# Quantizing the gate and up weights inside the attention stage, in tiles of 1024 columns, instead of in a stage of their own

## The chip, the cores and the metric

The kernel runs on all 8 cores of one Trainium2 chip. Each core takes half of one batch element: 1024 rows of the output, with the other 1024 rows of its batch element as keys and values. All weights are given to every core, and every core does all the weight preparation for itself. The metric is the device time of the slowest core in microseconds. Of the kernel before there are three timed runs (60560.01, 60564.8 and 60569.77 us, median 60564.8 us) and one profiled execution.

TensorE (PE in the profile) multiplies matrices and transposes, VectorE (DVE) and ScalarE (ACT) work element by element, GpSimd (POOL) and SyncE (SP) only issue DMAs here. Each engine works through its own queue in program order.

## The reference

A layer norm of x gives xn, then two branches are added to x:

```
q, k, v = xn @ Wq.T + bq, ...              # 16 heads of 256
logits  = (q_rev*met) @ k.T / 16 + (q_rev @ wk[h]) @ k.T
attn    = softmax(logits) @ v
gate    = mxq(xn, 3 bits) @ mxq(w_gate, 1 bit).T      # w_gate, w_up: [11008, 4096]
up      = mxq(xn, 3 bits) @ mxq(w_up, 1 bit).T
ffn     = mxq(silu(gate)*up, 3 bits) @ mxq(w_down, 1 bit).T
y       = x + attn + ffn
```

`mxq` works on blocks of 32 values along the contraction: it finds the largest magnitude of a block, takes the power of two below it as a shared scale, and rounds each scaled value to the nearest of a few values (0, 0.5, 1, 1.5, 2, 3, 4, 6 with a sign for 1 bit of mantissa). Since a block has 32 values, a row can be quantized in pieces of any multiple of 32 columns.

## The kernel before

There are four stages, with a barrier of all engines and queues between them. Their places on the time axis are those of the slowest core.

- **Stage 1** (to about 1600 us, lines 260 to 349): layer norm of 16 tiles of 128 rows; each tile is transposed into `s_xnT` in DRAM. For the core's own 8 tiles, `_emit_quant` also quantizes the row in two pieces of 2048 columns, with the working tiles `QT` (`q_...` in the profile).
- **Stage 2** (to about 15280 us, lines 351 to 526): the attention, one head at a time. A head first casts its q, k and v weights on DVE (12 casts of 128x2048, from the double-buffered `wstage`). Then comes a loop over four slices of 512 positions (`tc`): PE multiplies the `xnc` tiles with the weights, 32 steps to a slice, ACT evicts `kh` and `qtmp`, DVE evicts `vh`. PE then makes `qeff`. Then comes a loop over 8 tiles of 128 queries (`qt`): logits on PE, maximum (`nm`) on DVE, exponential on ACT, transposes on PE, copies on DVE, product with v on PE, and a scaled copy to `ostg` on DVE, which POOL stores into `s_attn`.
- **Stage 3** (to about 42340 us, lines 528 to 594): the weights. For each 128-row tile of `wg` and `wu` (86 row tiles each, 4096 columns) and of `wd` (32 row tiles, 11008 columns), pieces of 2048 (for `wd` 2752) columns of float32 are loaded by SP into one of two `win` tiles, quantized by `_emit_quant` on DVE and ACT into `wqrt`, transposed by PE in batches of 8 blocks of 128x128, copied by DVE from PSUM to `tstg3`, and stored by POOL.
- **Stage 4** (lines 596 to 736): gate and up products, silu, quantization of the product in 1024 columns (working tiles `QT4`, `f_...` in the profile), transposes, and the down product, four times for 256 rows.

The order of the work on an engine is the order in which the Python code emits it. `Eng.op` (line 31) lets each instruction of DVE, ACT and PE wait for the one before it on its own engine, so there is no overlap of two instructions within an engine. `Stream.dma` (line 50) issues a DMA on SP or POOL; `qwait` (line 232) puts a wait into the queue of SP or POOL, and everything that is emitted later on that queue stays behind it.

`_emit_quant` (line 100) with `mbits` 1 is, on DVE: a block maximum, 50 small instructions on one value for each block, a multiplication into `zt`; then ACT makes `sgn` and `at` (absolute value) from `zt` while DVE waits; then 11 more instructions on DVE over all columns. Only `sgn`, `at` and `zt` tie it to ACT.

Of the kernel before, what the change touches and what calls it, by code (L numbers as in the profile page):

```python
# [7 lines left out]
F32 = mybir.dt.float32  # L8
BF16 = mybir.dt.bfloat16
# [4 lines left out]
D = 4096  # L14
# [4 lines left out]
I = 11008  # L19
# [161 lines left out]
def build_nc():  # L181
# [18 lines left out]
    s_wgT = nc.dram_tensor("s_wgT", [D, I], BF16, kind="Internal").ap()  # L200
    s_wuT = nc.dram_tensor("s_wuT", [D, I], BF16, kind="Internal").ap()
    s_wdT = nc.dram_tensor("s_wdT", [I, D], BF16, kind="Internal").ap()

    ctx = ExitStack()
    with ctx:
# [3 lines left out]
        def sem(name):  # L209
            return ctx.enter_context(nc.semaphore(name))  # L210
# [50 lines left out]
        with p1:  # L261
            def sb1(name, shape, dt=F32):
                return p1.enter_context(nc.sbuf_tensor(name, shape, dt))
# [4 lines left out]
            xnq_t = sb1("xnq_t", [128, D], BF16)  # L268
            tstage = [sb1("tstage%d" % i, [128, 1024], BF16) for i in range(2)]
            psT = [p1.enter_context(nc.psum_tensor("psT%d" % i, [128, 1024], BF16)) for i in range(2)]  # L270
            QT = {
                "am": sb1("q_am", [128, 64], F32), "b1": sb1("q_b1", [128, 64], F32),
                "b2": sb1("q_b2", [128, 64], F32), "b3": sb1("q_b3", [128, 64], F32),
                "b4": sb1("q_b4", [128, 64], F32), "b5": sb1("q_b5", [128, 64], F32),
                "zt": sb1("q_zt", [128, 2048], F32), "at": sb1("q_at", [128, 2048], F32),
                "u2": sb1("q_u2", [128, 2048], F32),
                "cA": sb1("q_cA", [128, 2048], BF16), "cB": sb1("q_cB", [128, 2048], BF16),
                "cC": sb1("q_cC", [128, 2048], BF16), "cD": sb1("q_cD", [128, 2048], BF16),
                "cE": sb1("q_cE", [128, 2048], BF16), "cF": sb1("q_cF", [128, 2048], BF16),
                "sgn": sb1("q_sgn", [128, 2048], BF16),  # L280
            }

            t.wait(lds.sem, small_ld)
            xnT_v = s_xnT.rearrange("p (a c) -> p a c", a=32)
# [24 lines left out]
            for tt in range(NTILE):  # L309
                par = tt % 2  # L310
                qwait(nc.sync, ssem, buf_free[par])
                ldm = ldx[par].dma(xt2[par][:], xb[tt*128:(tt+1)*128, :])
                v.wait(ldx[par].sem, ldm)
                s.wait(ldx[par].sem, ldm)
                v.op("reduce_sum", lnS[:], xt2[par][:], AX.X)
                s.op("activation", sqscr[:], xt2[par][:], ACT.Square, accum_out=lnQ[:])
                sqm = s.n
                v.wait(ssem, sqm)
                v.op("tensor_single_scalar", lnM[:], lnS[:], 1.0 / D, ALU.mult)
                v.op("tensor_single_scalar", lnE[:], lnQ[:], 1.0 / D, ALU.mult)  # L320
# [12 lines left out]
                s.op("activation", xnf[:], xt2[par][:], ACT.Identity, bias=lnB[:], scale=lnR[:])
                s.op("activation", xnb[:], xnf[:], ACT.Identity)
                buf_free[par] = s.n
                xnm = s.n
                t.wait(ssem, xnm)
                emit_transpose_out(xnb, xnT_v, tt)
                if tt < NOWN:
                    v.wait(ssem, xnm)  # L340
                    for cc in range(2):
                        _emit_quant(v, s, xnf[:, cc*2048:(cc+1)*2048], 2048, 3, QT,
                                    xnq_t[:, cc*2048:(cc+1)*2048])
                    xqm = v.n
                    t.wait(vsem, xqm)
                    emit_transpose_out(xnq_t, xnqT_v, tt)
# [5 lines left out]
        with p2:  # L352
# [47 lines left out]
            for h in range(NH):  # L400
# [3 lines left out]
                for wname, wview, wbuf in (("q", wqT_v, wq_bf), ("k", wkT_v, wk_bf), ("v", wvT_v, wv_bf)):  # L404
# [8 lines left out]
                        wfree_v[wp] = v.n  # L413
                    wcast[wname] = v.n
                t.wait(vsem, max(wcast.values()))
                for tc in range(4):
                    for dc in range(32):
                        par = dc % 2
# [35 lines left out]
                    evV = v.n  # L454
                    t.wait(ssem, evK)
                    t.wait(vsem, evV)
                for cc in range(2):
                    for nn in range(2):
                        t.op("matmul", ps[0][:], th_all[:, h*128:(h+1)*128],
                             qtmp[:, cc*LQ + nn*512: cc*LQ + nn*512 + 512], start=True, stop=True)  # L460
                        trm = t.n
                        s.wait(tsem, trm)
                        s.op("activation", qeff[:, cc*LQ + nn*512: cc*LQ + nn*512 + 512],
                             ps[0][:], ACT.Identity)
                        t.wait(ssem, s.n)
                qeffm = s.n
                t.wait(ssem, qeffm)
                for qt in range(8):
                    for kc in range(4):
                        for cc in range(2):  # L470
# [37 lines left out]
                    for kc in range(16):  # L508
# [10 lines left out]
                    sto[opar].dma(s_attn[qt*128:(qt+1)*128, h*HD:(h+1)*HD], ostg[opar][:])  # L519
                    pmark[("ost", opar)] = sto[opar].cnt  # L520
                    pmark["attn_cons"] = t.n
                pmark["kh_cons"] = t.n
            p2_marks = [(vsem, v.n), (ssem, s.n), (tsem, t.n),
                        (ldw[0].sem, ldw[0].cnt), (ldw[1].sem, ldw[1].cnt), (ld2s.sem, ld2s.cnt),
                        (ldc[0].sem, ldc[0].cnt), (ldc[1].sem, ldc[1].cnt),
                        (sto[0].sem, sto[0].cnt), (sto[1].sem, sto[1].cnt)]

        p3 = ExitStack()
        with p3:
# [21 lines left out]
            psT3_free = [0, 0]  # L551
            qcons = 0

            for wdram, wscr, R, Cw in ((wg, s_wgT, I, D), (wu, s_wuT, I, D), (wd, s_wdT, D, I)):
                csz = 2752 if Cw % 2752 == 0 else 2048
                wscr_v = wscr.rearrange("(a p) c -> p a c", p=128)
                for rt in range(R // 128):
                    for cc in range(Cw // csz):
                        par = (rt * (Cw // csz) + cc) % 2
                        qwait(nc.sync, vsem, in_free[par])  # L560
                        ldm = ld3[par].dma(win[par][:, 0:csz], wdram[rt*128:(rt+1)*128, cc*csz:(cc+1)*csz])
                        v.wait(ld3[par].sem, ldm)
                        s.wait(ld3[par].sem, ldm)
                        def qg(qcons=qcons):
                            v.wait(tsem, qcons)
                        _emit_quant(v, s, win[par][:, 0:csz], csz, 1, QT3,
                                    wqrt[:, cc*csz:(cc+1)*csz], qgate=qg)
                        in_free[par] = v.n
                    qdone = v.n
                    t.wait(vsem, qdone)  # L570
                    nk = Cw // 128
                    for batch in range((nk + 7) // 8):
                        bpar = batch % 2
# [23 lines left out]
        with p4:  # L597
            def sb4(name, shape, dt=F32):
# [4 lines left out]
            wsl = [sb4("wsl%d" % i, [128, 32 * 512], BF16) for i in range(2)]  # L603
            sgt = sb4("sgt", [128, 1024], F32)
            intf = sb4("intf", [128, 1024], F32)
            QT4 = {
                "am": sb4("f_am", [128, 32], F32), "b1": sb4("f_b1", [128, 32], F32),
                "b2": sb4("f_b2", [128, 32], F32), "b3": sb4("f_b3", [128, 32], F32),
                "b4": sb4("f_b4", [128, 32], F32), "b5": sb4("f_b5", [128, 32], F32),
                "zt": sb4("f_zt", [128, 1024], F32), "at": sb4("f_at", [128, 1024], F32),  # L610
                "u2": sb4("f_u2", [128, 1024], F32),
                "cA": sb4("f_cA", [128, 1024], BF16), "cB": sb4("f_cB", [128, 1024], BF16),
                "cC": sb4("f_cC", [128, 1024], BF16), "cD": sb4("f_cD", [128, 1024], BF16),
                "cE": sb4("f_cE", [128, 1024], BF16), "cF": sb4("f_cF", [128, 1024], BF16),
                "sgn": sb4("f_sgn", [128, 1024], BF16),
            }
# [30 lines left out]
            for tt2 in range(4):  # L647
# [4 lines left out]
                for ici in range(NIC):  # L652
# [31 lines left out]
                    ev_marks["mul"] = v.n  # L684
                    def qg4():
                        v.wait(tsem, iq_free)
                    _emit_quant(v, s, intf[:, 0:2*isz], 2 * isz, 3, QT4, iq[:, 0:2*isz], qgate=qg4)
                    iqm = v.n
                    t.wait(vsem, iqm)
                    t.wait(vsem, psTr_free)  # L690
# [99 lines left out]
```

How the kernel before makes its waits and increments, by code:

```python
    def op(self, method, *args, **kw):  # L31
        if self.n > 0:
            self.e.wait_ge(self.sem, self.n)
        inst = getattr(self.e, method)(*args, **kw)
        inst.then_inc(self.sem, 1)
        self.n += 1
        return inst
# [1 line left out]
    def wait(self, sem, count):  # L39
        if count > 0:
            self.e.wait_ge(sem, count)
# [8 lines left out]
    def dma(self, out, in_):  # L50
        self.q.dma_start(out=out, in_=in_).then_inc(self.sem, 16)
        self.cnt += 16
        return self.cnt
# [1 line left out]
    def dmaT(self, out, in_):  # L55
        self.q.dma_start_transpose(out=out, in_=in_).then_inc(self.sem, 16)
        self.cnt += 16
        return self.cnt
# [122 lines left out]
def build_nc():  # L181
# [50 lines left out]
        def qwait(q, semh, val):  # L232
            if val > 0:
                q.wait_ge(semh, val)
# [490 lines left out]
                        v.wait(sty[ypar].sem, yst_free[ypar])  # L725
                        v.op("tensor_tensor", yst[ypar][:], psD[tc][:], xres[:], ALU.add)
                        v.op("tensor_tensor", yst[ypar][:], yst[ypar][:], ares[:], ALU.add)
                        res_free = v.n
                        ym = v.n
                        qwait(nc.gpsimd, vsem, ym)
                        sty[ypar].dma(y[row0:row0+128, dcD*512:(dcD+1)*512], yst[ypar][:])
                        yst_free[ypar] = sty[ypar].cnt
                    t.wait(vsem, res_free)
                iqT_free = t.n
            nc.sync.wait_ge(sty[0].sem, sty[0].cnt)
            nc.sync.wait_ge(sty[1].sem, sty[1].cnt)
    return nc
```

## Time and profile before

| | |
|---|---|
| median of three runs | 60564.8 us |
| the profiled execution's own time | 60516.05 us |
| its span on the slowest core (core 0) | 60515.0 us |
| spans of the eight cores | 60432.7 to 60515.0 us |
| granted TensorE clock, all cores | 1.000 |
| DVE busy | 23785.4 us, 39% |
| PE busy | 20771.3 us, 34% |
| ACT busy | 3052.9 us, 5% |
| POOL busy | 1114.4 us, 2% |
| HBM traffic | 41 GB/s over the span |

No engine is busy most of the time, and the memory is far from busy. The work is a chain: an instruction ends, the next one on the same or another engine starts. The share of busy time of an engine says little here; what counts is which engine holds the chain in a given stage. Line 34 is the helper `Eng.op`, so nearly all instructions have that line, and the profile is read by tile names. Line 51 is the helper that issues DMAs.

### The profile page before, as it was taken

Reading aid. Unit: us, or ns where it says so; the run is one execution under the profiler, and the core shown is the slowest. Engines: PE = TensorE matmul, PEld = TensorE weight load, DVE = VectorE, ACT = ScalarE, POOL = GpSimd, SP = SyncE. Lnnn points to the kernel's source line nnn. Section 1 sums busy time; section 2 is a strip of 40 time slices with the busy share of each in tenths; the row PEclk is TensorE's granted clock in tenths of the full one; section 3 lists DMA queues with packets and bytes.
Section 4 is the critical chain, followed back from the end, with each engine's and each line's share of the span. In section 5 each row is a group of like instructions: output and inputs, shape, how many; then the busy total and the mean of one; then the engine's idle time right before and its main releaser. Section 6 shows DMA issues by size and latency. Waiting matters only on the chain.

```text
span 60515.0 us, 254596 instructions; the slowest of 8 cores (60432.7 to 60515.0 us)
## 1 busy us (share of the span) xinstructions
PE 20771.3 (34%) x46000; PEld 4828.0 (8%) x46000; DVE 23785.4 (39%) x41288; ACT 3052.9 (5%) x2691; POOL 1114.4 (2%) x1332
## 2 busy tenths in 40 slices
PE   1666666666100000000000000000555555555555
PEld 0111111111000000000000000000100001001101
DVE  6000000000666666666666777766220220220220
ACT  1000000000000000000000000000000000000000
POOL 0000000000000000000000000000000000000000
DMA  1111111111000100000011111111112112112212
GB/s 36 43 36 37 32 40 35 37 37 32 28 29 29 29 29 29 29 29 29 29 29 29 31 32 32 31 33 34 63 56 66 64 59 66 64 59 67 66 56 68
DMA packets 1823659, 2516.91 MB, mean 42 GB/s; under 512 B 114464, under 2 KB 1662752, under 8 KB 1759648
## 3 DMA queue, kind: packets, MB, share of 16 engines
q1 hardware_dynamic: 1720608, 2171.28, 11.3%
q0 software_dynamic: 101632, 329.34, 2.2%
q8 instruction: 570, 9.34, 0.1%
q14 instruction: 849, 6.96, 0.0%
HBM read 2170.90 MB, written 329.25 MB: 41 GB/s over the span
## 4 chain that ended last, share of the span: by engine, by line
DVE 38%; PE 33%; issue 16%; DMA 7%; ACT 5%; DVEq 1%; SPq 0%; ACTq 0%; POOL 0%; POOLq 0%
PE ps L34 12%; DVE p_b L34 9%; DVE p_cB L34 8%; DVE p_cA L34 7%; DMA wdsl<-s_wdT 5%; PE psT L34 4%; PE psQ L34 3%; PE psD L34 3%; PE psA L34 3%; PE psC L34 3%; PE psB L34 3%; PE psDD L34 3%; DVE p_zt L34 2%; DVE wqrt L34 2%; DVE p_am L34 2%
## 5 line engine op out<-in xcount | busy, mean ns | idle before, releaser
L34 PE MATMUL psT<-idn_sb,wqrt 128*128 128x128 bf16 x8256 | 2171.8, 263 | 24890.2 <-DVE wqrt L34 23679.8
L34 PE MATMUL psD<-wdsl,iqT 128*128 128x512 bf16 x5504 | 3213.4, 584 | 2481.2 <-DMA wdsl<-s_wdT 1697.9
L34 DVE TENSOR_TENSOR vh<-ps,bv_sb 128x256 bf16<-128x256 f32 x256 | 108.8, 425 | 8855.2 <-PE psQ L34 5164.4
L34 DVE SCALAR_TENSOR_TENSOR p_cA<-p_at,p_cA 128x2048 bf16<-128x2048 f32 (+1 forms) x1416 | 3527.1, 2491 | 150.4 <-DVE p_cA L34 4.1
L34 PE MATMUL ps<-wv_bf,xnc 128*128 128x256 bf16 x8192 | 3031.0, 370 | 1229.5 <-PE ps L34 101.6
L34 DVE TENSOR_TENSOR intf<-sgt,psC 128x512 f32<-128x512 f32 x88 | 59.5, 676 | 8320.5 <-ACT sgt L34 8320.5
L34 PEld LDWEIGHTS psT<-idn_sb,wqrt 128*128 128x128 bf16 x8256 | 866.6, 105 | 26195.5 <-issue 26195.5
L34 PE MATMUL ps<-xnc,wk_bf 128*128 128x512 bf16 x4096 | 2388.2, 583 | 1575.1 <-DVE wv_bf L34 802.5
L34 DVE TENSOR_SCALAR p_b<-p_b 128x64 f32<-128x64 f32 (+1 forms) x11800 | 2340.3, 198 | 1297.0 <-DVE p_b L34 62.6
L34 DVE TENSOR_TENSOR p_b<-p_b 128x64 f32<-128x64 f32 (+1 forms) x9912 | 2296.9, 232 | 1070.7 <-DVE p_b L34 54.7
L34 DVE TENSOR_TENSOR yst<-psD,xres 128x512 f32<-128x512 f32 x64 | 44.3, 692 | 5629.5 <-DMA ares<-s_attn 4261.3
L34 ACT ACTIVATE p_sgn<-p_zt 128x2048 bf16<-128x2048 f32 (+1 forms) x472 | 976.2, 2068 | 25017.9 <-DVE p_zt L34 25017.9
L34 DVE COPY tstg<-psT 128x1024 bf16<-128x1024 bf16 (+1 forms) x1040 | 714.9, 687 | 2929.7 <-PE psT L34 2927.6
L34 PE MATMUL psA<-wsl,xnq_tt 128*128 128x512 bf16 (+1 forms) x2816 | 1614.8, 573 | 549.7 <-PE psA L34 125.3
L34 PE MATMUL psDD<-wsl,xnq_tt 128*128 128x512 bf16 (+1 forms) x2816 | 1614.5, 573 | 423.3 <-PE psDD L34 131.5
L34 PE MATMUL psB<-wsl,xnq_tt 128*128 128x512 bf16 (+1 forms) x2816 | 1614.5, 573 | 423.3 <-PE psB L34 131.8
L34 PE MATMUL psC<-wsl,xnq_tt 128*128 128x512 bf16 (+1 forms) x2816 | 1614.5, 573 | 423.3 <-PE psC L34 129.9
L34 PE MATMUL psTr<-idn_sb,iq 128*128 128x128 bf16 x688 | 181.2, 263 | 4013.8 <-DVE iq L34 3923.7
L34 DVE TENSOR_SCALAR p_cA<-p_at 128x2048 bf16<-128x2048 f32 (+1 forms) x472 | 626.1, 1326 | 2153.4 <-ACT p_at L34 2153.4
L34 PE MATMUL psQ<-xnc,wq_bf 128*128 128x512 bf16 x2048 | 1194.0, 583 | 307.5 <-PE psQ L34 50.6
L34 DVE TENSOR_TENSOR p_zt<-win,p_b 128x2048 f32<-128x2048 f32 (+1 forms) x472 | 1176.0, 2491 | 52.7 <-DVE p_b L34 5.0
L34 DVE SCALAR_TENSOR_TENSOR p_cB<-p_cA,p_cB 128x2048 bf16<-128x2048 bf16 (+1 forms) x472 | 1175.6, 2491 | 51.6 <-DVE p_cC L34 3.2
(138 smaller groups left out, 21055.7 us busy)
## 6 DMA issues: line engine op xcount, KB each, us to landing
wdsl<-s_wdT SPq DMA_DIRECT2D x2752, 128.0 KB, 2.2
wsl<-s_wgT SPq DMA_DIRECT2D x84, 4096.0 KB, 13.7
wsl<-s_wuT SPq DMA_DIRECT2D x84, 4096.0 KB, 13.6
xnc<-s_xnT SPq DMA_DIRECT2D x2048, 128.0 KB, 2.0
win<-wg SPq DMA_DIRECT2D x172, 1024.0 KB, 5.0
win<-wu SPq DMA_DIRECT2D x172, 1024.0 KB, 5.0
win<-wd SPq DMA_DIRECT2D x128, 1376.0 KB, 5.6
s_wgT<-tstg POOLq DMA_DIRECT2D x344, 256.0 KB, 3.2
```

Of the source, the lines that this page charges most:

```text
L34: inst = getattr(self.e, method)(*args, **kw)
```

## The change

Stage 3 for `wg` and `wu` is split in two. Their quantization moves into stage 2, as 688 tasks of 128x1024 (86 row tiles x 4 pieces x 2 matrices), whose results go to two new DRAM tensors `s_wgq` and `s_wuq`. Stage 3 then loads a quantized row of bfloat16 straight into `wqrt` and only transposes it. The tasks are emitted by `qtask(n)`: four before a head's loop over `tc`, three after the evictions of each slice, two before its loop over `qt`, one after the store of `ostg` of every odd query tile, and all that are left after the last head. `wd` keeps its old path. The 1024-column working tiles `QTG` replace `QT` and `QT4`, so stage 1 quantizes in four pieces of 1024 columns instead of two of 2048; stage 4 does what it did, in the new tiles.

```diff
+        qld = [Stream(nc.gpsimd, sem("qld%d" % i)) for i in range(2)]
+        qst = [Stream(nc.gpsimd, sem("qst%d" % i)) for i in range(2)]
...
+        def qtask(n):
+            for _ in range(n):
+                ti = qstate["i"]
+                if ti >= len(wq_tiles):
+                    return
+                qstate["i"] += 1
+                wdram_, wscr_, rt_, cc_ = wq_tiles[ti]
+                par = ti % 2
+                qwait(nc.gpsimd, vsem, qstate["in_free"][par])
+                ldm = qld[par].dma(win2[par][:],
+                                   wdram_[rt_*128:(rt_+1)*128, cc_*1024:(cc_+1)*1024])
+                v.wait(qld[par].sem, ldm)
+                s.wait(qld[par].sem, ldm)
+                def qg(par=par):
+                    v.wait(qst[par].sem, qstate["st_mark"][par])
+                _emit_quant(v, s, win2[par][:], 1024, 1, QTG, qsg[par][:], qgate=qg)
+                qstate["in_free"][par] = v.n
+                qwait(nc.gpsimd, vsem, v.n)
+                qst[par].dma(wscr_[rt_*128:(rt_+1)*128, cc_*1024:(cc_+1)*1024], qsg[par][:])
+                qstate["st_mark"][par] = qst[par].cnt
...
-                    for cc in range(2):
-                        _emit_quant(v, s, xnf[:, cc*2048:(cc+1)*2048], 2048, 3, QT,
+                    for cc in range(4):
+                        _emit_quant(v, s, xnf[:, cc*1024:(cc+1)*1024], 1024, 3, QTG,
...
                 t.wait(vsem, max(wcast.values()))
+                qtask(4)
...
                     t.wait(vsem, evV)
+                    qtask(3)
...
                 t.wait(ssem, qeffm)
+                qtask(2)
...
+                    if qt % 2 == 1:
+                        qtask(1)
                 pmark["kh_cons"] = t.n
+            qtask(len(wq_tiles))
...
+                qwait(nc.sync, tsem, qcons)
                 for rt in range(R // 128):
...
+                    if prequant:
+                        par = rt % 2
+                        qwait(nc.sync, tsem, qcons)
+                        ldm = ld3[par].dma(wqrt[:, 0:Cw], wdram[rt*128:(rt+1)*128, :])
+                        t.wait(ld3[par].sem, ldm)
```

The first place is the queue of POOL in the first head: before, the stores of `ostg` stand one behind the other.

```order
100 L51 DMA s_attn<-ostg0 128x256 [waits vsem,ssem,tsem,lds,ldx0,ldx1,stt0,stt1]
101 L51 DMA s_attn<-ostg1 128x256 [waits vsem]
102 L51 DMA s_attn<-ostg0 128x256 [waits vsem]
103 L51 DMA s_attn<-ostg1 128x256 [waits vsem]
104 L51 DMA s_attn<-ostg0 128x256 [waits vsem]
```

Now the same queue holds the loads (`win2`) and the stores (`qsg`) of the tasks; these rows are the last tasks before the query loop of the first head, and the first task within it.

```order
131 L51 DMA s_wgq<-qsg1 128x1024 [waits vsem]
132 L51 DMA win2_0<-wg 128x1024 [waits vsem]
133 L51 DMA s_wgq<-qsg0 128x1024 [waits vsem]
134 L51 DMA win2_1<-wg 128x1024 [waits vsem]
135 L51 DMA s_wgq<-qsg1 128x1024 [waits vsem]
136 L51 DMA s_attn<-ostg0 128x256 [waits vsem]
137 L51 DMA s_attn<-ostg1 128x256 [waits vsem]
138 L51 DMA win2_0<-wg 128x1024 [waits vsem]
139 L51 DMA s_wgq<-qsg0 128x1024 [waits vsem]
140 L51 DMA s_attn<-ostg0 128x256 [waits vsem]
```

The load of a task stands behind the store of the task before it, which waits for DVE to finish that task.

The second place is DVE at the end of the last slice of the first head and at the first query tile. Before, the maximum follows the eviction of `vh`.

```order
1434 L34 TENSOR_TENSOR vh<-ps4,bv_sb 128x256
1435 L34 TENSOR_TENSOR vh<-ps5,bv_sb 128x256
1436 L34 TENSOR_REDUCE nm<-ps0 128x1
1437 L34 TENSOR_REDUCE nm<-ps1 128x1
1438 L34 TENSOR_REDUCE nm<-ps2 128x1
```

Now five tasks stand between them (61 rows each; the first and the last row of the outer ones are shown), and one task stands between `ostg` of an odd query tile and the maximum of the next.

```order
3364 L34 TENSOR_TENSOR vh<-ps5,bv_sb 128x256 [waits vsem]
3365 L34 TENSOR_REDUCE g_am<-win2_1 128x32 [waits qld1,vsem]
...
3609 L34 TENSOR_REDUCE g_am<-win2_1 128x32 [waits qld1,vsem]
...
3669 L34 TENSOR_TENSOR qsg1<-g_cB,g_b5 128x1024 [waits qst1,vsem]
3670 L34 TENSOR_REDUCE nm<-ps0 128x1 [waits tsem,vsem]
...
3693 L34 TENSOR_SCALAR ostg1<-ps5,rr 128x256 [waits tsem,vsem]
3694 L34 TENSOR_REDUCE g_am<-win2_0 128x32 [waits qld0,vsem]
...
3754 L34 TENSOR_TENSOR qsg0<-g_cB,g_b5 128x1024 [waits qst0,vsem]
3755 L34 TENSOR_REDUCE nm<-ps0 128x1 [waits tsem,vsem]
```

So 60 instructions or more of DVE now stand where nothing stood. A head has 4 + 4x3 + 2 + 4 = 22 tasks, so the 16 heads take 352 of the 688; the last call takes the other 336, with no other work beside them.

## Rows read from the trace of the kernel before

**Rows 1.** The page: the span, and the costliest wait of a group.

```profile
span 60515.0 us, 254596 instructions; the slowest of 8 cores (60432.7 to 60515.0 us)
...
L34 PE MATMUL psT<-idn_sb,wqrt 128*128 128x128 bf16 x8256 | 2171.8, 263 | 24890.2 <-DVE wqrt L34 23679.8
```

**Rows 2.** Busy time by stretch, us (instructions): stage 2, then stage 3's gate and up.

```profile
1600.00:15260.00 13660.00, 8535.04 (x19490) 2045.95 (x19490) 1099.24 (x2301) 569.60 (x1281) 74.22 (x127) 1.00 0.12 36
15260.00:33870.00 18610.00, 1454.57 (x5523) 579.71 (x5523) 12786.48 (x22361) 1313.52 (x688) 607.92 (x687) 1.00 0.10 29
```

**Rows 3.** Timeline, DVE, one gate row tile: start us, duration us, instruction.

```profile
20039.83 2.29 DVE L34 TENSOR_REDUCE p_am<-win 128x64 f32<-128x2048 f32 x1
...
20131.19 2.29 DVE L34 TENSOR_TENSOR wqrt<-p_cB,p_b 128x2048 bf16<-128x2048 bf16 x1
...
20147.96 2.29 DVE L34 TENSOR_REDUCE p_am<-win 128x64 f32<-128x2048 f32 x1
```

**Rows 4.** Timeline, PE, first and last of the 32 transposes of a row tile.

```profile
20025.71 0.26 PE L34 MATMUL psT<-idn_sb,wqrt 128*128 128x128 bf16 x1 [95.04 <-DVE wqrt L34]
...
20038.53 0.26 PE L34 MATMUL psT<-idn_sb,wqrt 128*128 128x128 bf16 x1 [0.15 <-PE psT L34]
```

**Rows 5.** Timeline, DVE, a 1024-column quantization of stage 4.

```profile
45030.10 1.22 DVE L34 TENSOR_REDUCE f_am<-intf 128x32 f32<-128x1024 f32 x1
...
45049.97 0.69 DVE L34 TENSOR_SCALAR f_cA<-f_at 128x1024 bf16<-128x1024 f32 x1 [2.52 <-ACT f_at L34]
45050.77 0.69 DVE L34 TENSOR_SCALAR f_cB<-f_at 128x1024 bf16<-128x1024 f32 x1
...
45052.10 1.23 DVE L34 SCALAR_TENSOR_TENSOR f_cC<-f_cB,f_cC 128x1024 bf16<-128x1024 bf16 x1
45053.43 1.23 DVE L34 TENSOR_TENSOR f_u<-f_at,f_cC 128x1024 f32<-128x1024 f32 x1
...
45070.45 1.23 DVE L34 TENSOR_TENSOR iq<-f_cD,f_b 128x1024 bf16<-128x1024 bf16 x1
```

**Rows 6.** Timeline, DVE, one head of stage 2.

```profile
4199.33 2.56 DVE L34 CAST wq_bf<-wstage 128x2048 bf16<-128x2048 f32 x2
...
4243.42 1.23 DVE L34 CAST wv_bf<-wstage 128x2048 bf16<-128x2048 f32 x1 [1.48 <-DMA wstage<-wvT]
4405.46 2.01 DVE L34 TENSOR_TENSOR vh<-ps,bv_sb 128x256 bf16<-128x256 f32 x4 [160.81 <-PE psQ L34]
...
4686.47 2.01 DVE L34 TENSOR_TENSOR vh<-ps,bv_sb 128x256 bf16<-128x256 f32 x4 [115.03 <-PE ps L34]
4803.55 2.01 DVE L34 TENSOR_TENSOR vh<-ps,bv_sb 128x256 bf16<-128x256 f32 x4 [115.07 <-PE ps L34]
4818.17 3.07 DVE L34 TENSOR_REDUCE nm<-ps 128x1 f32<-128x512 f32 x4 [12.62 <-PE ps L34]
...
4842.09 0.48 DVE L34 TENSOR_SCALAR ostg<-ps,rr 128x256 f32<-128x256 f32 x1 [8.78 <-PE ps L34]
4847.89 3.08 DVE L34 TENSOR_REDUCE nm<-ps 128x1 f32<-128x512 f32 x4 [5.31 <-PE ps L34]
```

**Rows 7.** Timeline, POOL, the store of that `ostg`.

```profile
4843.11 0.54 POOL L51 DMA_DIRECT2D s_attn<-ostg  x1 [642.43 <-DVE ostg L34]
```

**Rows 8.** DMA issues: count, KB each, median us from issue to landing.

```profile
xnc<-s_xnT SPq DMA_DIRECT2D x2048, 128.0 KB, 2.0
win<-wg SPq DMA_DIRECT2D x172, 1024.0 KB, 5.0
...
xres<-xb SPq DMA_DIRECT2D x64, 256.0 KB, 3.1
...
y<-yst POOLq DMA_DIRECT2D x64, 256.0 KB, 4.1
```

**Rows 9.** Timeline, DVE, two quantizations of stage 1, one after the other.

```profile
42.56 2.29 DVE L34 TENSOR_REDUCE q_am<-xnf 128x64 f32<-128x2048 f32 x1
...
105.58 2.29 DVE L34 TENSOR_REDUCE q_am<-xnf 128x64 f32<-128x2048 f32 x1
```

More of the change, by code:

```diff
@@ L202, in build_nc @@
     s_wdT = nc.dram_tensor("s_wdT", [I, D], BF16, kind="Internal").ap()
+    s_wgq = nc.dram_tensor("s_wgq", [I, D], BF16, kind="Internal").ap()
+    s_wuq = nc.dram_tensor("s_wuq", [I, D], BF16, kind="Internal").ap()
     ctx = ExitStack()
@@ L253, in build_nc @@
         rr = sb("rr", [128, 1], F32)
+        QTG = {
+            "am": sb("g_am", [128, 32], F32), "b1": sb("g_b1", [128, 32], F32),
+            "b2": sb("g_b2", [128, 32], F32), "b3": sb("g_b3", [128, 32], F32),
+            "b4": sb("g_b4", [128, 32], F32), "b5": sb("g_b5", [128, 32], F32),
+            "zt": sb("g_zt", [128, 1024], F32), "at": sb("g_at", [128, 1024], F32),
+            "u2": sb("g_u2", [128, 1024], F32),
+            "cA": sb("g_cA", [128, 1024], BF16), "cB": sb("g_cB", [128, 1024], BF16),
+            "cC": sb("g_cC", [128, 1024], BF16), "cD": sb("g_cD", [128, 1024], BF16),
+            "cE": sb("g_cE", [128, 1024], BF16), "cF": sb("g_cF", [128, 1024], BF16),
+            "sgn": sb("g_sgn", [128, 1024], BF16),
+        }
+        win2 = [sb("win2_%d" % i, [128, 1024], F32) for i in range(2)]
+        qsg = [sb("qsg%d" % i, [128, 1024], BF16) for i in range(2)]
+        wq_tiles = []
+        for wdram_, wscr_ in ((wg, s_wgq), (wu, s_wuq)):
+            for rt_ in range(I // 128):
+                for cc_ in range(4):
+                    wq_tiles.append((wdram_, wscr_, rt_, cc_))
+        qstate = {"i": 0, "in_free": [0, 0], "st_mark": [0, 0]}
+        def qtask(n):
[18 more added lines that the diff above has]
+                qstate["st_mark"][par] = qst[par].cnt
         lds.dma(idn_sb[:], idn)
@@ L270, in build_nc @@
             psT = [p1.enter_context(nc.psum_tensor("psT%d" % i, [128, 1024], BF16)) for i in range(2)]
[L271 to L281, printed above, removed]
             t.wait(lds.sem, small_ld)
@@ L340, in build_nc @@
                     v.wait(ssem, xnm)
-                    for cc in range(2):
-                        _emit_quant(v, s, xnf[:, cc*2048:(cc+1)*2048], 2048, 3, QT,
-                                    xnq_t[:, cc*2048:(cc+1)*2048])
+                    for cc in range(4):
+                        _emit_quant(v, s, xnf[:, cc*1024:(cc+1)*1024], 1024, 3, QTG,
+                                    xnq_t[:, cc*1024:(cc+1)*1024])
                     xqm = v.n
@@ L525, in build_nc @@
                         (ldc[0].sem, ldc[0].cnt), (ldc[1].sem, ldc[1].cnt),
-                        (sto[0].sem, sto[0].cnt), (sto[1].sem, sto[1].cnt)]
+                        (sto[0].sem, sto[0].cnt), (sto[1].sem, sto[1].cnt),
+                        (qld[0].sem, qld[0].cnt), (qld[1].sem, qld[1].cnt),
+                        (qst[0].sem, qst[0].cnt), (qst[1].sem, qst[1].cnt)]
         p3 = ExitStack()
@@ L552, in build_nc, with qg @@
             qcons = 0
-            for wdram, wscr, R, Cw in ((wg, s_wgT, I, D), (wu, s_wuT, I, D), (wd, s_wdT, D, I)):
+            for wdram, wscr, R, Cw in ((s_wgq, s_wgT, I, D), (s_wuq, s_wuT, I, D), (wd, s_wdT, D, I)):
+                prequant = wdram is not wd
                 csz = 2752 if Cw % 2752 == 0 else 2048
                 wscr_v = wscr.rearrange("(a p) c -> p a c", p=128)
+                qwait(nc.sync, tsem, qcons)
                 for rt in range(R // 128):
[L558 to L570, printed above, removed]
+                    if prequant:
[3 more added lines that the diff above has]
+                        t.wait(ld3[par].sem, ldm)
+                    else:
+                        for cc in range(Cw // csz):
+                            par = (rt * (Cw // csz) + cc) % 2
+                            qwait(nc.sync, vsem, in_free[par])
+                            ldm = ld3[par].dma(win[par][:, 0:csz], wdram[rt*128:(rt+1)*128, cc*csz:(cc+1)*csz])
+                            v.wait(ld3[par].sem, ldm)
+                            s.wait(ld3[par].sem, ldm)
+                            def qg(qcons=qcons):
+                                v.wait(tsem, qcons)
+                            _emit_quant(v, s, win[par][:, 0:csz], csz, 1, QT3,
+                                        wqrt[:, cc*csz:(cc+1)*csz], qgate=qg)
+                            in_free[par] = v.n
+                        qdone = v.n
+                        t.wait(vsem, qdone)
                     nk = Cw // 128
@@ L605, in build_nc @@
             intf = sb4("intf", [128, 1024], F32)
[L606 to L616, printed above, removed]
             iq = sb4("iq", [128, 1024], BF16)
@@ L686, in qg4 @@
                         v.wait(tsem, iq_free)
-                    _emit_quant(v, s, intf[:, 0:2*isz], 2 * isz, 3, QT4, iq[:, 0:2*isz], qgate=qg4)
+                    _emit_quant(v, s, intf[:, 0:2*isz], 2 * isz, 3, QTG, iq[:, 0:2*isz], qgate=qg4)
                     iqm = v.n
```

## The prediction

> **What bounds the kernel now.** I read the page first: no engine is busy more than 39%, and of the waits the largest by far is PE's in stage 3, where the transposes of `wqrt` wait 23.7 ms for DVE [rows 1]. The busy time by stretch then says who holds the chain where: in the stretch of gate and up, DVE works 12.8 of 18.6 ms and PE 1.5; in the attention it is the reverse, PE works 8.5 of 13.7 ms and DVE 1.1 [rows 2]. Read alone, this invites laying the one beside the other. So I went to the timelines, to see where in a head DVE is idle and PE is not: only in the four slices, where DVE waits 160.8 us (the first two) and 115.0 us (the last two) for PE [rows 6]. In the query loop DVE's waits are short (5.3 us before the maximum), and PE waits for DVE and ACT in turn [rows 6]: there is no cover there. In stage 3 one row tile takes 147.96 - 39.83 = 108.1 us [rows 3].
>
> **What goes away: the quantization of gate and up in stage 3.** Before, 172 row tiles x 108.1 = 18.60 ms. After, a row tile is one load, then 32 transposes, in series, since `wqrt` is a single buffer and SP waits for the last transpose. The transposes take 20038.79 - 20025.71 = 13.1 us [rows 4]. The load has the size and row length of `win<-wg`, 5.0 us [rows 8]. Two hand-overs cost about 0.5 us together (one from DVE to POOL took 43.11 - 42.57 = 0.54 [rows 6, 7]). That is 18.6; I take 19.0, since the last stores of the row before land beside the load. The copies on DVE and the stores run beside the transposes as they did. 172 x 19.0 = 3.27 ms. Gone: 15.33 ms. Bounds: 18.1 us without hand-overs, and 24 us if load and hand-overs double; so -0.15 to +0.86 ms.
>
> **A task by itself.** No 1024-column task with 1 bit is in the trace, but stage 4 quantizes 1024 columns, and everything up to the first comparison is the same code: 45049.97 - 45030.10 = 19.9 us, with the wait for ACT in it [rows 5]. After it come 11 instructions: four of the kind that recurs every 0.80 us (three comparisons and the sign product) and seven that recur every 1.33 us [rows 5]. So 19.87 + 4 x 0.80 + 7 x 1.33 - 0.10 = 32.3 us. A piece of 2048 columns takes (20133.48 - 20039.83) / 2 = 46.8 us [rows 3], so two tasks cost 64.6 where one piece cost 46.8: the 50 small instructions do not shrink with the columns. This is the first thing that speaks against the change.
>
> **The gap between tasks.** The second is on POOL. A task's load stands behind the store of the task before, which waits until DVE is done. There are two `win2` tiles, but the order of the queue makes them one: DVE ends, 0.54 us later POOL issues the store, which takes 0.54 [rows 7], then the load (0.2 for the step between), then it lands, then DVE starts (0.15). The landing of 512 KB: 256 KB take 3.1 us and 1024 KB 5.0 [rows 8], so 3.7 on a line between, and 0.3 more for the store just ahead: 4.0. Gap: 5.4 us. Period in a series: 32.3 + 5.4 = 37.7 us. Bounds for the gap: 4.2 (landing 3.1, no step) and 10.7 (the step another 0.54, the store's 4.1 wholly ahead of a 5.0 landing [rows 8]). I take 5.4 because the load is nearest to the plain loads of rows 8.
>
> **Stage 2, one head.** The first load of a group was issued when the group before ended, so a group of n costs 32.3 + (n-1) x 37.7.
> - Four tasks beside slice 0: 145.4 us under 160.8. Three beside each later slice: 107.7 under 160 and under 115.0. All hidden, 13 tasks a head, with 7.3 us to spare in the tightest. ACT's share is done before its evictions are due.
> - Three after the last slice and two before the query loop: five in a row on DVE, 183.1 us, where there were 12.6 us of waiting [rows 6]. ACT's `qeff` evictions stand behind three tasks, but all of that is inside the 183.1. Exposed: 170.5.
> - After query tiles 1, 3 and 5: the load is issued only after the store of `ostg`, so gap and task both show: 5.4 + 32.3 + 0.1 = 37.8, against 5.3 us of waiting before: +32.5 each, 97.5. PE can do one set of logits in that time and then waits.
> - After query tile 7: `ostg` was followed by the casts at once (4199.33, `vh`'s weights done at 4244.65, PE starts) [rows 6]. The task goes ahead of them: +37.8.
>
> Sum for a head 305.8, for 16 heads 4.89 ms. The extra loads go past the `xnc` loads: a step of PE in the last slices takes 117.1 / 32 = 3.66 us, an `xnc` load 2.0 [rows 6, 8], so there are 1.6 us of cover; moving 512 KB takes about 1.3 us (1.9 us for 768 KB [rows 8]). I count nothing; without cover 26 transfers x 1.3 x 16 = 0.5 ms.
>
> **After the last head.** 336 tasks in series with nothing beside them: 336 x 37.7 = 12.67 ms.
>
> **Stage 1.** Quantizing with 3 bits: 2048 columns took 105.58 - 42.56 = 63.0 us [rows 9], 1024 columns 41.7 (45030.10 to 45071.68 and 0.1 [rows 5]). 8 x (4 x 41.7 - 2 x 63.0) = 0.33 ms, on DVE, which holds the chain there; at least 0 if it were hidden. Stage 4 and `wd` stay as they are.
>
> **Sum.** 0.33 + 4.89 + 12.67 - 15.33 = +2.56 ms. The profiled execution took 60516 us, which gives 63076; it lies 49 us under the median of the runs, so I forecast 63120 us, 4.2% slower. In short: 480 of 688 tasks have no cover, and each costs 37.7 us where its share of the old stage, half of 46.8, was 23.4 us; hiding the other 208 does not pay for that.
>
> The Trainium skill has a figure for such a transfer (DMA: Bandwidth & Descriptors, Anatomy of one DMA — SWDGE (gpsimd) path): about 2.0 us and the bytes at 436 GB/s. By it 512 KB would land in an estimated 3.2 us, 0.8 less than I take, and with 464 exposed gaps the total would be 0.37 ms lower, 62750. The rows are above the page for the same sizes (5.0 us for 1024 KB from SP where it gives an estimated 4.4, 4.1 for 256 KB from POOL where it gives 2.6 [rows 8]), so I stay with the rows.
>
> **The rivals.** Each us of gap is worth 464 us: 336 in the tail and in each head four inside the group of five and four after odd query tiles (128).
> - *Store and load one after the other.* The load waits for the store to be done, gap about 9.8. For it: both are on POOL's one queue, and 256 KB stores take 4.1 us. Against: `xnc` loads are in flight two at a time. It gives 4.4 x 464 = +2.04 ms, and the groups of three would take 116.5, 1.5 over, x 32 = 0.05: 65210. Chance 9%.
> - *Crowding.* The transposing stage takes 24 us a row and the `xnc` loads lose their cover: +0.86 + 0.5: 64480, or half of it. For it: the row now moves its 2 MB in 19 us. Against: in the old stage the DMA engines were busy 0.10 of 108 us for 3 MB [rows 2], 11 us, so they would be under 60% busy. Chance 12%.
> - *The load is ready when DVE ends, not slower.* If the second `win2` tile did prefetch, all 464 gaps would go: -2.51 ms, which gives +0.05 ms, 60615, no change. The change is slower for any gap above zero, so this rival needs the whole gap gone, and a gain needs the task below 32.3 us besides (480 x 1 us = 0.48 ms). For it: there are two tiles, with semaphores of their own. Against: the order of POOL's queue, in which no load precedes the store of the task before. Chance 6%.
>
> The sum as worked out has 73%, with its own range 62500 to 63900 (gap 4.2 to 6.5, the row tile 18.1 to 20, stage 1 from 0). For 8 times in 10 I reach toward the upper rivals: 62300 to 64600. A measurement of this kernel can tell 0.2% (120 us) from no change. The 6% of the last rival are split evenly between just faster and the same: faster 3%, same 3%, slower 94%.
>
> **What the profile will show.** Right: the attention lasting about 13.65 + 4.9 = 18.6 ms, then a stretch of 12.7 ms in which only DVE and ACT work, with `g_am` of one task 37.7 us after that of the one before; DVE's waits for `win2` loads of 5.4 us, 464 of them; slices as long as before (160.8 and 115.0); row tiles of 19 us with PE waiting for `wqrt<-s_wgq`; from then on the same times as before. Wrong: `win2` loads issued while DVE is still in the task before; slices longer than before; a period in the tail of under 34 or over 41 us; row tiles over 22 us. The forecast as a whole is wrong if the tail lasts under 11 ms, since no other term is large enough to turn the sign.

## The result, and the profile after

The change makes the kernel 4.5% slower: a median of 63241.75 us (63113.9 to 63406.16, 8 runs) against 60539.66 us (60508.07 to 60569.77, 8 runs), ratio 1.0446, 95% interval 1.0435 to 1.0458. The forecast was 63120 us, the range 62300 to 64600. The profiled execution of the changed kernel has its slowest core in core 6, with a span of 63240.9 us, 2725.9 over the 60515.0 of before. The borders of the stages are read from the first and last instruction on a tile (the load of `bv_sb`, the last `ostg`, the first load of `wqrt` or `win`, the first `p_am` of `wd`):

| stage | before | after | difference | forecast |
|---|---|---|---|---|
| layer norm and 3-bit quantization | 1600.7 | 1923.9 | +323 | +330 |
| 16 heads, to the last `ostg` | 13674.6 | 18595.3 | +4921 | +4855 |
| tasks after the last `ostg` (337) | 3.2 | 12856.7 | +12854 | +12705 |
| gate and up in stage 3 | 18597.2 | 3233.2 | -15364 | -15330 |
| `wd` and stage 4 | 26639.3 | 26631.8 | -8 | 0 |
| sum | 60515.0 | 63240.9 | +2726 | +2560 |

(The task after the last query tile is counted by the forecast with the heads; here it stands in the third row, so 38 us are moved.)

First the page of the changed kernel, its costliest wait of PE (busy us, mean ns, then idle us before, and who ended it). It answers to [rows 1].

```profile
L34 PE MATMUL psT<-idn_sb,wqrt 128*128 128x128 bf16 x8256 | 2173.6, 263 | 22378.1 <-DMA wqrt<-s_wgq 13345.2
```

Of PE's 23.7 ms of waiting for DVE before this line, 16.35 ms belonged to gate and up and 7.33 ms to `wd`, which did not change. Most of the part of gate and up is still there (13.83 ms), under a new name: 13345 us are now put down to the loads of `s_wgq` and 487 us to those of `s_wuq`, and 12862 us are one single wait, the first, which is the tail in which DVE still quantizes. The name alone would mislead to the DMA.

The busy time by stretch: the heads, the tail, then gate and up in stage 3 (us, busy us of PE, PEld, DVE, ACT, POOL with counts, clock, DMA share, GB/s).

```profile
1925.00:20520.00 18595.00, 8548.62 (x19520) 2051.46 (x19520) 9136.40 (x24417) 1311.14 (x1983) 461.57 (x828) 1.00 0.14 42
20520.00:33376.00 12856.00, 0.00 (x0) 0.00 (x0) 7715.09 (x21231) 711.83 (x674) 361.42 (x675) 1.00 0.07 21
33376.00:36609.00 3233.00, 1449.22 (x5504) 578.28 (x5504) 475.51 (x688) 0.00 (x0) 609.52 (x688) 1.00 0.39 112
```

In the heads DVE's work rose by 8 ms against [rows 2], and the stretch by only 4.9: so much of it lies beside PE. In the tail PE does nothing at all, and the DMA engines are 7% busy. It is a chain of one engine with its small gaps. In the last stretch a row tile takes 3233 / 172 = 18.8 us.

DVE in the tail, one task and the start of the next (start us, duration us, instruction, idle before it and who ended it):

```profile
25022.05 1.22 DVE L34 TENSOR_REDUCE g_am<-win 128x32 f32<-128x1024 f32 x1 [5.40 <-DMA win<-wu]
...
25041.73 0.69 DVE L34 TENSOR_SCALAR g_cA<-g_at 128x1024 bf16<-128x1024 f32 x1 [2.52 <-ACT g_at L34]
...
25052.89 1.23 DVE L34 TENSOR_TENSOR qsg<-g_cB,g_b 128x1024 bf16<-128x1024 bf16 x1
25060.53 1.22 DVE L34 TENSOR_REDUCE g_am<-win 128x32 f32<-128x1024 f32 x1 [6.41 <-DMA win<-wu]
```

The task takes 25054.12 - 25022.05 = 32.07 us, as composed from [rows 5] (32.3), and the gap is 5.4 to 6.4 us. POOL in the same piece shows where the gap is from:

```profile
25017.19 0.54 POOL L51 DMA_DIRECT2D s_wuq<-qsg  x1 [37.37 <-DVE qsg L34]
25017.72 0.54 POOL L51 DMA_DIRECT2D win<-wu  x1
25054.65 0.54 POOL L51 DMA_DIRECT2D s_wuq<-qsg  x1 [36.39 <-DVE qsg L34]
25055.18 0.54 POOL L51 DMA_DIRECT2D win<-wu  x1
```

DVE ends at 25054.12, the store is issued 0.53 us later, the load another 0.53 later, and the next task starts 5.35 after that. There are two `win2` tiles, yet not one of the 688 loads is under way while DVE works on a task.

The end of a head's last slice and its first query tiles, on DVE. It answers to [rows 6], where `vh` and `nm` had 12.6 us between them.

```profile
4911.72 2.01 DVE L34 TENSOR_TENSOR vh<-ps,bv_sb 128x256 bf16<-128x256 f32 x4 [5.58 <-PE ps L34]
4915.45 1.22 DVE L34 TENSOR_REDUCE g_am<-win 128x32 f32<-128x1024 f32 x1 [1.72 <-DMA win<-wg]
...
5098.36 3.08 DVE L34 TENSOR_REDUCE nm<-ps 128x1 f32<-128x512 f32 x4
...
5152.01 0.48 DVE L34 TENSOR_SCALAR ostg<-ps,rr 128x256 f32<-128x256 f32 x1 [8.78 <-PE ps L34]
5157.96 1.22 DVE L34 TENSOR_REDUCE g_am<-win 128x32 f32<-128x1024 f32 x1 [5.47 <-DMA win<-wg]
5190.32 3.07 DVE L34 TENSOR_REDUCE nm<-ps 128x1 f32<-128x512 f32 x4
```

From the end of `vh` to the maximum there are now 184.6 us (forecast 183.1), and from the end of `ostg` of an odd tile to the next maximum 37.8 (forecast 37.8). The idle time of 5.58 us before `vh` is the margin of the tightest slice; 7.3 had been worked out.

The landings, in the form of [rows 8]:

```profile
win<-wu POOLq DMA_DIRECT2D x344, 512.0 KB, 4.7
...
s_wuq<-qsg POOLq DMA_DIRECT2D x344, 256.0 KB, 3.9
wqrt<-s_wgq SPq DMA_DIRECT2D x86, 1024.0 KB, 5.2
```

### The profile page after: what moved, and what is told of

It is laid out like the page before. It is cut to its first block, busy times and chain, and to the rows that moved or that the text cites. A ratio compares the mean times of both kernels' runs of the same rounds, so it can differ in the third digit from the quotient of the medians.

```text
span 63240.9 us, 305895 instructions; the slowest of 8 cores (63104.0 to 63240.9 us)
## 1 busy us (share of the span) xinstructions
PE 20779.9 (33%) x46000; PEld 4832.8 (8%) x46000; DVE 27410.2 (43%) x64128; ACT 3199.2 (5%) x3411; POOL 1863.2 (3%) x2708
## 4 chain that ended last, share of the span: by engine, by line
DVE 36%; PE 29%; issue 16%; DMA 12%; ACT 4%; DVEq 2%; POOL 0%; SPq 0%; ACTq 0%; POOLq 0%
DVE g_b L34 10%; PE ps L34 9%; DMA wdsl<-s_wdT 5%; DVE g_cB L34 4%; PE psT L34 4%; DVE g_cA L34 4%; PE psQ L34 3%; PE psD L34 3%; PE psA L34 3%; PE psB L34 3%; PE psDD L34 3%; PE psC L34 3%; DMA win<-wu 3%; DVE p_cB L34 2%; DVE p_b L34 2%
## 5 line engine op out<-in xcount | busy, mean ns | idle before, releaser
L34 DVE TENSOR_SCALAR g_b<-g_b 128x32 f32<-128x32 f32 x20200 | 3655.9, 181 | 2224.4 <-DVE g_b L34 112.4
L34 DVE TENSOR_TENSOR g_b<-g_b 128x32 f32<-128x32 f32 (+1 forms) x16968 | 3256.5, 192 | 1837.2 <-DVE g_b L34 96.0
L34 DVE SCALAR_TENSOR_TENSOR g_cA<-g_at,g_cA 128x1024 bf16<-128x1024 f32 x2064 | 2528.3, 1225 | 221.2 <-DVE g_cA L34 8.3
L34 DVE TENSOR_REDUCE g_am<-win 128x32 f32<-128x1024 f32 x688 | 839.1, 1220 | 3631.9 <-DMA win<-wu 2056.4
L34 ACT ACTIVATE g_sgn<-g_zt 128x1024 bf16<-128x1024 f32 (+1 forms) x808 | 851.7, 1054 | 27279.0 <-DVE g_zt L34 27155.6
L34 PE MATMUL psQ<-idn_sb,attn 128*128 128x128 bf16 x2048 | 539.5, 263 | 4094.6 <-DVE ssum L34 3672.7
L34 DVE TENSOR_SCALAR g_cA<-g_at 128x1024 bf16<-128x1024 f32 (+1 forms) x808 | 559.6, 693 | 2044.9 <-ACT g_at L34 2044.9
L34 DVE SCALAR_TENSOR_TENSOR p_cA<-p_at,p_cA 128x2752 bf16<-128x2752 f32 x384 | 1161.6, 3025 | 41.4 <-DVE p_cA L34 1.8
```

Of the source, the lines that this page charges most:

```text
L34: inst = getattr(self.e, method)(*args, **kw)
```

## The experiments

Three theories stood: the uncovered work costs by itself (a missing cover), the narrow pieces make more of it (width), and POOL's queue adds a gap to each task (queue). The total could come out right with these terms wrong against each other, so each was taken alone.

**Load a task ahead.** `qload(ti)` is the wait and the load of the task, taken out of `qtask`; everything else is as in the changed kernel.

```diff
+                ldm = qstate["ld_mark"][par]
+                qload(ti + 1)
                 v.wait(qld[par].sem, ldm)
                 ...
                 qwait(nc.gpsimd, vsem, v.n)
                 qst[par].dma(...)
```

> The changed kernel, but the load of the next task is issued on POOL at the start of the task before it, ahead of that task's store. Theory of the queue (POOL's order makes two win2 tiles one, and each of 464 uncovered tasks waits about 6.0 us for its load: DVE's idle time before g_am is 3625 us for some 608 waits): the wait before g_am goes, the tail's period falls from 38.2 to 32.4 us, and the total by 464 x 6.0 = 2.8 ms to about 60.5 ms. Rival, the transfer itself is too slow under load or holds up the engines (crowding): the period stays above 35 us and the total above 61.5 ms. Rival, the wait is only put down to the load and something else on DVE takes it: total stays near 63.2 ms.

60603.92 us median, ratio to the kernel before 1.0006, interval 0.9996 to 1.0015: no difference from the kernel before. DVE in the tail:

```profile
25014.77 1.22 DVE L34 TENSOR_REDUCE g_am<-win 128x32 f32<-128x1024 f32 x1
...
25045.81 1.23 DVE L34 TENSOR_TENSOR qsg<-g_cB,g_b 128x1024 bf16<-128x1024 bf16 x1
25047.14 1.22 DVE L34 TENSOR_REDUCE g_am<-win 128x32 f32<-128x1024 f32 x1
```

No idle time is left before `g_am`; the period is 32.4 us and the tail 10878 us. The theory of the queue holds, and the whole loss of the change against the kernel before is these 464 gaps. This does not make them the only cause: without them the cover that the change wins is just eaten by the width (by an estimate, the 208 hidden tasks of 32.3 us are 6.7 ms; the width costs 6.4 ms in the run with narrow pieces below).

**Load before store.** In the same code `qload(ti + 1)` stands between the last `qwait` and the store.

> The changed kernel, but when a task ends POOL issues the load of the next one first and the store of the finished one second. The gap was 6.0 us and I had worked out 5.4, with 0.54 for the store's issue and 4.0 for the landing. If the store ahead costs its issue time only, the gap falls by 0.54 us, 464 x 0.54 = 0.25 ms, to 62.99 ms. If the store's data also hold up the load, the landing falls too, from 4.6 toward 3.7 us: gap 4.6, total about 62.6 ms. If neither matters, 63.24 ms.

62803.16 us, ratio to before 1.0373 (1.0355 to 1.039), about 440 us less than the change. This expectation overlooked that the edit also issues the load of a query-loop task long before its `ostg`, so those 64 tasks lose their whole wait, and the heads are 0.29 ms shorter (18305 us against 18595). The tail is free of that: 12675 us against 12856, 181 less, as much as 336 x 0.54, the issue of one store for each load. POOL shows load and store in turn, and on the slowest core, core 1, the landing is 4.6 us where the changed kernel's slowest core had 4.7:

```profile
win<-wu POOLq DMA_DIRECT2D x344, 512.0 KB, 4.6
```

These are two different cores, though, core 6 there and core 1 here. On core 0 the landing became longer, first in the changed kernel, then in this run:

```profile
win<-wu POOLq DMA_DIRECT2D x344, 512.0 KB, 4.2
```

```profile
win<-wu POOLq DMA_DIRECT2D x344, 512.0 KB, 4.7
```

There the mean wait for these loads fell only from 5.57 to 5.47 us. Cores 0 to 5 all show this: the load lands 0.2 to 0.4 us later when the store is issued right behind it than when the store is issued right ahead of it. Only cores 6 and 7, which waited longest in the changed kernel, gain the whole 0.54. So the new order saves the issue of a store, and on most cores a longer landing gives back half of that or more (one profiled execution of each kernel); why was not tried. The 0.3 us that I had put into the landing for a store ahead of the load are not shown to come from that store, since with the store behind it the load lands no earlier.

**Narrow pieces, nothing moved.** The kernel before with

```diff
-                csz = 2752 if Cw % 2752 == 0 else 2048
+                csz = 2752 if Cw % 2752 == 0 else 1024
```

and stage 1 in four pieces of 1024.

> The kernel before, nothing moved, but stage 1 and gate and up in stage 3 quantize in pieces of 1024 columns instead of 2048. Theory of the width (50 small instructions and the wait for ACT are paid again for each piece): a piece costs 32.4 us, so a row tile 4 x 32.4 + 14.4 = 144.0 instead of 108.1 us; 172 x 35.9 = 6.17 ms, and stage 1 gets 0.33 ms longer: 67.0 ms. Rival, the width costs little and the loss of the change is the gaps and the missing cover alone: under 62 ms.

66951.57 us, ratio 1.1056 (1.1034 to 1.1078). Two maxima that each start a row tile:

```profile
20062.09 1.22 DVE L34 TENSOR_REDUCE p_am<-win 128x32 f32<-128x1024 f32 x1
...
20205.55 1.22 DVE L34 TENSOR_REDUCE p_am<-win 128x32 f32<-128x1024 f32 x1
```

143.5 us where [rows 3] had 108.1. The width alone, with stage 1, costs 6.4 ms when nothing hides it. Stage 1 ends at 1923.7 us, as in the changed kernel (1923.9): its +323 us are the width, and nothing else.

**Tasks only in the slices.** The changed kernel without the tasks after the last slice, before the query loop and in it; the tail has 480.

```diff
-                    qtask(3)
+                    if tc < 3:
+                        qtask(3)
...
-                qtask(2)
...
-                    if qt % 2 == 1:
-                        qtask(1)
```

> The changed kernel with only those 13 tasks of a head that lie beside a slice of PE work; the other nine of each head are done in the tail, which has 480 tasks instead of 336. Theory (an uncovered task costs the same wherever it stands, less the short waits it fills): the heads get shorter by 4.96 ms, back to 852 us each as before, the tail longer by 144 x 38.2 = 5.50 ms; total 63.8 ms. Rival, tasks inside the query loop cost more than themselves, since they hold up ACT and PE as well: the total falls below 63.2 ms. Rival, the 13 are not free either: heads longer than 860 us.

63843.72 us, ratio to before 1.054 (1.0525 to 1.0556). The busy time of the heads and of the tail, on its slowest core:

```profile
1924.60:15616.00 13691.40, 8563.42 (x19520) 2048.96 (x19520) 5865.45 (x15408) 1009.56 (x1697) 308.76 (x543) 1.00 0.16 48
15616.00:33835.00 18219.00, 0.00 (x0) 0.00 (x0) 10992.53 (x30241) 1013.89 (x960) 514.54 (x961) 1.00 0.07 21
```

The heads took 13691 us in all, 855.7 each, against 854.7 before; the tail 18219 us, 38.0 a task. A task in the query loop costs what it costs in the tail, less the wait that it fills, and the 13 in the slices cost 1 us a head.

**Only the covered part.** As above, but just the 208 tasks of the slices exist; the row tiles from the 53rd of `w_gate` on are quantized in stage 3 as before.

```diff
+        wq_tiles = wq_tiles[:208]
...
-            qtask(len(wq_tiles))
...
+                    prequant = wdram is wg and rt < 52
```

> The 13 tasks of a head beside the slices are kept (1024 columns, POOL's order as in the change: 208 tasks, the first 52 row tiles of w_gate); all other row tiles are quantized in stage 3 as before, in pieces of 2048. Theory (covered tasks are free, each row tile moved saves 108.1 - 18.75 us): 60540 + 320 for stage 1 - 52 x 89.4 = 56210 us, heads of 852 us. Rival, covered tasks slow the slices, since their loads delay the xnc loads or the stores hold up POOL: up to 0.5 ms more, 56.7 ms, with slices over 161 and 115 us. Rival, moving work to another stage brings nothing as such: 60.5 ms.

56344.79 us, ratio to before 0.93 (0.9286 to 0.9313). The heads, and the prequantized row tiles of stage 3:

```profile
1923.30:15706.00 13782.70, 8545.01 (x19520) 2048.95 (x19520) 5863.78 (x15408) 1009.04 (x1697) 308.70 (x543) 1.00 0.17 48
15709.00:16690.00 981.00, 437.77 (x1664) 174.66 (x1664) 143.80 (x208) 0.00 (x0) 184.29 (x208) 1.00 0.39 112
```

DVE did 4.8 ms more work in the heads than in [rows 2], and the heads became 0.1 ms longer. The prequantized row tiles took 981 us, 18.9 each. The total is 135 us over the 56210 expected, and most of that is in the heads. The heads took 13783 us, 861.4 each, 5.7 more than in the run before this one with the same code for them.

**Wide tasks, loaded ahead, covered only.** From the kernel before: tasks of 2048 columns with the load a task ahead, 3 before the first slice, then 3, 2 and 2; 80 row tiles of `w_gate`. Stage 1 and the rest of stage 3 stay as they were.

```diff
                 t.wait(vsem, max(wcast.values()))
+                qtask(3)
...
+                    if tc < 3:
+                        qtask(3 if tc == 0 else 2)
...
+                    if wdram is wg and rt < 80:
...
+                        ldm = ld3[par].dma(wqrt[:, 0:Cw], s_wgq[rt*128:(rt+1)*128, :])
```

> The kernel before with tasks of 2048 columns, each load issued a task ahead, placed only beside the slices (3, 3, 2, 2 a head, 160 tasks, 80 row tiles of w_gate); the rest in stage 3 as before and stage 1 as before. Theory: a task takes 46.9 us, so 140.7 fit under 160.8 and 93.8 under 115.0; 80 x 89.4 = 7.15 ms less than before: 53.4 ms. Rival, loads of 1 MB beside the xnc loads stretch the slices (crowding): 32 steps a slice, up to 1.5 us each for some: 53.9 to 54.5 ms. Rival, the casts at the head's start get later because the first load of a head stands beside the wstage loads: 16 x 10 us, 53.6 ms.

53695.59 us, ratio to before 0.8863 (0.8848 to 0.8877): 11.4% faster than the kernel before, and faster than every other version here. Here are two of its slices on DVE:

```profile
5177.66 2.29 DVE L34 TENSOR_REDUCE g_am<-win 128x64 f32<-128x2048 f32 x1
...
5315.99 2.29 DVE L34 TENSOR_TENSOR qsg<-g_cB,g_b 128x2048 bf16<-128x2048 bf16 x1
5341.69 2.01 DVE L34 TENSOR_TENSOR vh<-ps,bv_sb 128x256 bf16<-128x256 f32 x4 [23.40 <-PE psQ L34]
5343.80 2.29 DVE L34 TENSOR_REDUCE g_am<-win 128x64 f32<-128x2048 f32 x1
...
5505.80 2.01 DVE L34 TENSOR_TENSOR vh<-ps,bv_sb 128x256 bf16<-128x256 f32 x4 [21.40 <-PE psQ L34]
```

Three tasks end 23 us before PE's slice does: DVE waits for PE, as it should. The 0.3 ms over the expectation are in the heads, 871.0 us each instead of 854.7. PE's waits for `xnc` (us in total, times, longest), first on core 0 of the kernel before, then on core 0 of the changed kernel, then on cores 0 and 5 of this one:

```profile
PE ps L34 <- DMA xnc<-s_xnT: 9.7, 17, 1.2
```

```profile
PE ps L34 <- DMA xnc<-s_xnT: 35.9, 49, 2.6
```

```profile
PE ps L34 <- DMA xnc<-s_xnT: 189.4, 125, 4.6
PE ps L34 <- DMA xnc<-s_xnT: 238.9, 157, 4.6
```

This is the crowding that I had as a rival: it exists, but PE's waits for `xnc` grew by only about 0.02 to 0.06 ms in the change, depending on the core, and by some 0.2 ms with loads of 1 MB.

**Tail loads from SP.** The changed kernel, with the 336 loads of the tail on SP's queue, behind the same wait for the task before.

```diff
-                qwait(nc.gpsimd, vsem, qstate["in_free"][par])
+                qwait(lq, vsem, v.n if tail else qstate["in_free"][par])
```

> The changed kernel, but in the tail the loads of the 336 tasks are issued from SP's queue; SP waits, as POOL did, until DVE has finished the task before, so nothing is loaded ahead. The gap came out at 6.0 us where 5.4 were worked out, and loading before the store took off only the store's issue time. Theory of the queue's own latency (a 512 KB load lands 3.4 us after its issue from SP, as in the kernel with narrow pieces, and 4.5 to 4.7 us from POOL): a landing of 3.4 to 3.6 us, a gap of 3.9, the tail 336 x 2.1 = 0.7 ms shorter, total 62.5 ms. Rival, in the tail the memory or the row pitch of these loads makes them slow from any queue (landing still 4.5): only the issue times of POOL and its later start go, 336 x 1.0 = 0.34 ms, total 62.9 ms. Rival, the time of a gap is not set by the load at all: 63.2 ms.

62577.56 us, ratio to before 1.033 (1.0313 to 1.0347). Its core 7 had 1545.5 us of waits for `win<-wu` in 344 (4.49 each) where the changed kernel's core 7 had 2057.8 (5.98 each). DVE, and the issues of SP and POOL (SP's row is three issues merged, of which the first starts at 25032.80, 0.07 us after DVE's end):

```profile
25031.50 1.23 DVE L34 TENSOR_TENSOR qsg<-g_cB,g_b 128x1024 bf16<-128x1024 bf16 x1
25037.01 1.22 DVE L34 TENSOR_REDUCE g_am<-win 128x32 f32<-128x1024 f32 x1 [4.28 <-DMA win<-wu]
```

```profile
25032.80 73.40 SPq L51 DMA_DIRECT2D win<-wu  x3
```

```profile
25033.26 0.54 POOL L51 DMA_DIRECT2D s_wuq<-qsg  x1 [36.31 <-DVE qsg L34]
```

Of the 1.49 us, 1.0 are the later start of the load on POOL (0.53 until POOL reacts instead of 0.07, and 0.53 for the store's issue), and 0.5 is the landing, 4.2 us instead of 4.7 on this core. Both theories were partly right: on SP the load lands 0.5 us earlier, not the 1.1 that the first theory had. The order changed with the queue, though: here the load is issued 0.46 us ahead of the store, in the changed kernel 0.53 behind it. With the load ahead of the store a load from POOL took 4.7 us on core 0 (the run with the load before the store) and one from SP 3.7, so what the queue alone makes of a landing lies between 0.5 and 1.0 us and is not settled.

## Why the prediction was right

**What bounds the kernel.** Right. The slices were the only cover: the run with tasks only in the slices shows 13 hidden tasks a head for 1 us. The other nine cost their full time wherever they stand, less the short waits that they fill (4.9 ms for 144 of them in the heads, 34 us each, against 38.0 in the tail).

**What goes away in stage 3.** Forecast -15.33 ms, measured -15.36. The row tile takes 18.8 us, between the 18.6 of the bare sum and the 19.0 that I took.

**A task by itself.** 32.3 us composed, 32.1 to 32.4 measured. Composing it from the same code at the same width in another stage was better than any scaling of the 2048-column pieces. The width as a cause is shown by the kernel with narrow pieces (+6.4 ms).

**The gap.** This is the term that was mis-sized: 5.4 us worked out, 5.98 measured (2056 us in 344 waits on core 6), and 149 of the 166 us that the forecast fell short are in the tail. Two parts were off. I gave 0.2 us to the step from store to load, and there is none. I gave 4.0 us to the landing, and it is 4.7 on the slowest core. The two errors are of opposite sign, so a part of the closeness is luck. On cores 0 to 5 the landing is 4.2 to 4.4 us and the gap in the tail 5.6 to 5.7. A line between the landings of 256 and 1024 KB from SP gave 3.7, and SP does land 512 KB in 3.7 us on cores 0 and 2 of the run with SP's loads; but from POOL, with the store ahead, it is 0.5 more (4.2 and 4.3 on those cores), and in these two profiled executions cores 6 and 7 are another 0.3 to 0.6 slower from either queue. That is not a property of these two cores: in the profiled execution of the run with tasks only in the slices, whose tail has the same code, the loads of `wu` land in 4.3 to 4.5 us on all eight, and over the recorded executions of the changed kernel the slowest core is 0, 2, 6 or 7. The metric follows the slowest core, and I had worked with medians of one core. Why a pair of cores is slower in an execution was not tried. The formula of the Trainium skill (DMA: Bandwidth & Descriptors, Anatomy of one DMA — SWDGE (gpsimd) path), which is given for DMAs issued from GpSimd, gives an estimated 3.2 us. The trace does not agree: such loads from POOL landed in 4.2 to 4.7 us in the tail, and those from SP in 3.4 at the least (the median in the kernel with narrow pieces; single loads there took as little as 3.0). The prediction also held the formula against a load from SP, for which it is not given.

**The heads.** +4855 forecast, +4921 measured: 66 us in 16 heads. A head's five tasks took 184.6 us instead of 183.1, which gives 24 of them, and PE's longer waits for `xnc` some 25 to 50. Nothing was counted for these although its bound of 0.5 ms stood in the text.

**The rivals.** Store and load one after the other: refuted. The gap would have been 9.8 us and was 5.6 to 6.0, and the load lands 4.2 to 4.7 us after its issue whether the store is issued just ahead of it or just behind. Crowding: real, and small. The load ready in time: what it would give was forecast as 60615 us, and the kernel that makes it true took 60604. The reason against it, the order of POOL's queue, was the right one: no load was under way during a task.

## What to carry to other kernels

Work moved to another stage is free only where the engine that takes it waits for another one, and that has to be read at each place of the timeline: the same DVE was idle 92% of the attention, but only four waits of a head were long enough to hold a task, and everything beyond them came back in full. Two buffers do not make a load early; what stands ahead of it in its queue decides, and an issue placed one step earlier was worth 2.6 ms here. When work is cut into smaller pieces to fit a gap, the part that does not shrink with the piece has to be paid again; the same move with wide pieces, loaded ahead and only as many as are covered, turned 4.5% slower into 11.4% faster.

## What the runs showed of the hardware that was not expected

A DMA issued from POOL starts 0.53 us after the instruction on DVE that it waits for, one from SP 0.07 us after, and in the tail 512 KB landed 4.2 us after the issue from POOL and 3.7 us after the issue from SP on core 0, with the store ahead of the load in the first case and behind it in the second. Two issues on POOL in a row follow each other after 0.53 us with nothing between. A load from POOL of the same size landed 4.2 us after its issue with the 256 KB store issued just ahead of it, and 4.7 us with the store just behind (core 0), and the store itself 3.4 and 5.0 us. In the profiled execution of the change, cores 6 and 7 waited longer for the same loads than the six others (4.7 against 4.2 to 4.4 us), and core 6 of these set the time; in other executions it was another core. And the same code for the heads took 855.7 us a head in one kernel and 861.4 in another, with PE waiting 36 and 87 us for `xnc` on core 0; the two differ only in what comes later, and the cause stays open.
